# A dense layer's up products as three products of rounded halves, for the last three of eight batches

## The reference

```python
# block 1, per batch of 1024 tokens
h  = layernorm(layernorm(x), gamma, beta)
h  = spiral_conv(h)                       # a causal convolution with a decaying complex exponential
x1 = h + layernorm(x)
h  = layernorm(x1, gamma, beta)
h  = silu(h @ w1 + b1) @ w2 + b2          # the dense layer: 128 -> 512 -> 128
x  = x + (h + x1)
# block 2: mixture of 8 experts, 2 for each token
logits = layernorm(x) @ router.T
top two experts a, b of each token, probabilities by softmax over the two logits
x = x + sum over a, b of prob * (gelu(layernorm(x) @ w1[e].T + b1[e]) @ w2[e].T + b2[e])
```

## Time and profile before

| | |
|---|---|
| median of 3 runs | 464.43 us (461.4, 464.46, 464.43) |
| the profiled execution's own time | 459.44 us |
| its span, first to last instruction | 457.7 us |
| busy: PE, DVE, ACT, POOL | 378.1 us (83%), 348.2 us (76%), 320.1 us (70%), 274.5 us (60%) |
| up products L825 | 128 records, 66.9 us |
| mean granted TensorE clock, as a share of full speed | 0.922 |
| batches 5, 6 and 7 of the dense layer | up products from 180.29 to 238.6 us of the span |

### The profile page before, as it was taken

The page is one execution under the profiler, slowest core; times in us unless marked ns, Lnnn a source line. Parts: engine busy times, 40 slices in busy tenths (PEclk is TensorE's granted clock), DMA queues, the critical chain, the costliest instruction groups (busy, mean ns, idle before and its releaser), DMA issues.

```text
span 457.7 us, 11199 instructions
## 1 busy us (share of the span) xinstructions
PE 378.1 (83%) x2716; PEld 323.4 (71%) x2716; DVE 348.2 (76%) x1320; ACT 320.1 (70%) x772; POOL 274.5 (60%) x339
## 2 busy tenths in 40 slices
PE   1275188797999899898994598999999999999970
PEld 1132147484867667685774588999999999999970
DVE  7999999796989988988438158776777777777770
ACT  5783386978888797976671555777777777777740
POOL 6980756393777788776746505675555555555451
PEclk9995589998989799999998579999999999999995
DMA  7649122020222221222312233444333333333200
GB/s 252 178 145 327 53 47 47 1 46 3 58 87 47 86 60 49 79 79 67 116 37 99 75 86 102 140 148 122 108 96 99 101 98 100 111 105 102 76 3 0
DMA packets 34434, 41.60 MB, mean 91 GB/s; under 512 B 5382, under 2 KB 29459, under 8 KB 34244
## 3 DMA queue, kind: packets, MB, share of 16 engines
q1 hardware_dynamic: 27236, 23.56, 17.9%
q0 software_dynamic: 7136, 17.33, 13.1%
HBM read 19.52 MB, written 18.92 MB: 84 GB/s over the span
## 4 chain that ended last, share of the span: by engine, by line
PE 59%; DVE 17%; issue 6%; POOL 5%; ACT 4%; POOLq 0%; DVEq 0%; ACTq 0%
PE up_p L998 12%; PE down_p L836 7%; PE up_p L825 7%; PE turn_p L998 6%; PE down_p L1017 6%; PE route_p L1017 6%; PE up_p L1017 5%; PE turn_p L813 4%; DVE stats L1097 3%; PE down_p L1007 2%; DVE work L1162 2%; DVE work L1160 2%; ACT work L648 2%; POOL sorted_rows L560 2%; PE route_p L874 2%
## 5 line engine op out<-in xcount | busy, mean ns | idle before, releaser
L597 POOL DMA_INDIRECT out<-result,out_id x91 | 89.2, 980 | 90.1 <-DVE result L1475 70.9
L560 POOL DMA_INDIRECT sorted_rows<-rows,pos x64 | 73.8, 1153 | 32.8 <-issue 16.8
L825 PE MATMUL up_p<-h_t,work 128*128 128x512 f32 x128 | 66.9, 651 | 10.5 <-ACT work L622 9.3
L836 PEld LDWEIGHTS down_p<-w_sb,work 128*128 128x128 f32 x512 | 60.6, 192 | 9.7 <-issue 9.6
L998 PE MATMUL up_p<-xt,work 128*128 128x128 f32 x488 | 66.5, 281 | 0.0
L787 ACT ACTIVATE work<-mw_c 128x256 f32 x182 | 65.6, 414 | 0.3 <-issue 0.2
L836 PE MATMUL down_p<-w_sb,work 128*128 128x128 f32 x512 | 63.0, 277 | 0.0
L998 PEld LDWEIGHTS up_p<-xt,work 128*128 128x128 f32 x488 | 61.0, 196 | 0.1
L772 ACT ACTIVATE hid_t<-up_p 128x512 f32<-128x512 f32 x61 | 36.4, 597 | 30.4 <-PE up_p L998 30.3
L813 PE MATMUL turn_p<-ident,work 128*128 128x128 f32 x192 | 30.2, 309 | 29.1 <-ACT work L648 11.9
L813 PEld LDWEIGHTS turn_p<-ident,work 128*128 128x128 f32 x192 | 25.7, 161 | 37.6 <-ACT work L648 12.8
(11 more groups left out here) (236 smaller groups left out, 812.9 us busy)
## 6 DMA issues: line engine op xcount, KB each, us to landing
tin<-sorted_rows SPq DMA_DIRECT2D x91, 136.0 KB, 2.2
resid<-in_x SPq DMA_DIRECT2D x8, 512.0 KB, 3.8
resid<-work POOLq DMA_DIRECT2D x8, 512.0 KB, 4.6
sorted_rows<-zeros SPq DMA_DIRECT2D x29, 136.0 KB, 2.3
out<-result,out_id POOLq DMA_INDIRECT x91
work<-in_mw SPq DMA_DIRECT2D x1, 1024.0 KB, 6.5
sorted_rows<-rows,pos POOLq DMA_INDIRECT x64, 2.5
work<-in_w SPq DMA_DIRECT2D x1, 256.0 KB
```

The costliest lines, as they stand in the source:

```text
L560: g.indirect_dma_start(sorted_dram, bass.IndirectOffsetOnAxis(pos[b % 2][:, j:j + 1], 0), rows[b % ROWBUFS][:, j, :], None).then_inc(s_sor ...
L597: g.indirect_dma_start(out_rows, bass.IndirectOffsetOnAxis(out_id[k][:, :], 0), result[k][:, :], None, bounds_check=TOKENS - 1, oob_is_err ...
L825: t.matmul(dst, w1_g[:, k], half(h_t, h), start=True, stop=True).then_inc(s_up, 1)
L836: last = t.matmul(down_p[:, j * D:(j + 1) * D], silu[c % 2][:, j * TILE:(j + 1) * TILE], w2_sb[:, c, :], start=False, stop=c == FC - 1, sk ...
```

## The change

For batches 5, 6 and 7 (`b >= SPLIT`, `SPLIT = 5`) each float32 up product becomes three f32r products that add up in the same PSUM tile: high half of `w1` with low half of `h`, high with high, low with high. ScalarE's `high(b)` writes the rounded `h_hi` in place of `h_t`. A new operation `low(b)` on VectorE subtracts `h_hi` from `turn_p` to get `h_lo`; it stands between `x2_sum(b-1)` and `x1_sum(b+1)`, and for batch 7 between `x2_sum(6)` and its statistics. The halves of the weights are made once: `w1_hi` by ScalarE at the end of its iteration 3, `w1_lo` by VectorE at the end of its iteration 4. The first products of a batch wait for `low(b)`, and `conv_turn(b+1)`, which overwrites `turn_p`, waits for it too. `h_t` moves to a slot of `work`, and `b2_hi` shares the space of `h_lo`.

```diff
+SPLIT = 5
...
+        h_hi = sb("h_hi", [128, LENGTH], f32r)
+        h_lo = sb("h_lo", [128, LENGTH], f32r)
+        w1_hi = sb("w1_hi", [128, FF], f32r)
+        w1_lo = sb("w1_lo", [128, FF], f32r)
+        b2_hi = h_lo[0:2, 0:HALF]
...
+        h_t = slot(16)
...
-                s_.activation(h_t[:, :], turn_p[:, :], ACT.Copy).then_inc(s_hi, 1)
+                s_.activation(h_t if b < SPLIT else h_hi[:, :], turn_p[:, :], ACT.Copy).then_inc(s_hi, 1)
...
                 if live(b3):
                     x0_norm(b3)
+                if i == 3:
+                    s_.activation(w1_hi[:, :], w1_g, ACT.Copy).then_inc(s_w1hi, 1)
...
                 if c == 0:
                     pe.wait_ge(s_hi, b + 1)
+                    if b >= SPLIT:
+                        pe.wait_ge(s_lo, b + 1 - SPLIT)
+                    if b == SPLIT:
+                        pe.wait_ge(s_w1lo, 1)
...
-                    t.matmul(dst, w1_g[:, k], half(h_t, h), start=True, stop=True).then_inc(s_up, 1)
+                    if b < SPLIT:
+                        t.matmul(dst, w1_g[:, k], half(h_t, h), start=True, stop=True).then_inc(s_up, 1)
+                        continue
+                    t.matmul(dst, w1_hi[:, k], half(h_lo, h), start=True, stop=False)
+                    t.matmul(dst, w1_hi[:, k], half(h_hi, h), start=False, stop=False)
+                    t.matmul(dst, w1_lo[:, k], half(h_hi, h), start=False, stop=True).then_inc(s_up, 1)
...
                 after(pe, s_hi, b)
+                if b > SPLIT:
+                    pe.wait_ge(s_lo, b - SPLIT)
                 turned(lambda j: vi[:, j * TILE:(j + 1) * TILE], s_t2)
...
+            def low(b):
+                v.wait_ge(s_hi, b + 1)
+                after(v, s_up, b * 2 * FC)
+                d.tensor_tensor(h_lo[:, :], turn_p[:, :], h_hi[:, :].bitcast(f32), ALU.subtract).then_inc(s_lo, 1)
...
                 if live(b0):
                     x2_sum(b0)
+                if i >= SPLIT:
+                    low(i)
                 if live(b1):
                     x1_sum(b1)
...
+                if i == SPLIT - 1:
+                    v.wait_ge(s_w1hi, 1)
+                    d.tensor_tensor(w1_lo[:, :], w1_g, w1_hi[:, :].bitcast(f32), ALU.subtract).then_inc(s_w1lo, 1)
...
             x2_sum(LAST - 1)
+            low(LAST)
             x2_stats(LAST - 1)
```

More of the change, by code:

```diff
@@ L93, in block_moe_kernel @@
         ident = sb("ident", [128, 128])
-        h_t = sb("h_t", [128, LENGTH])
-        b2_hi = sb("b2_hi", [2, HALF], f32r)
+        h_hi = sb("h_hi", [128, LENGTH], f32r)
[3 more added lines that the diff above has]
+        b2_hi = h_lo[0:2, 0:HALF]
         mw1_c = sb("mw1_c", [128, EXPERTS * EF])
@@ L293, in block_moe_kernel @@
         s_hi = sem("h_turned_copied")
+        s_lo = sem("h_low_half_ready")
+        s_w1hi = sem("w1_high_ready")
+        s_w1lo = sem("w1_low_ready")
         s_up = sem("up_done")
@@ L731, in _ @@
             a.wait_ge(s_ident, 1)
-            s_.activation(b2_hi[:, :], b2_rows, ACT.Copy).then_inc(s_aw, 1)
+            s_.activation(b2_hi, b2_rows, ACT.Copy).then_inc(s_aw, 1)
             s_.activation(w1_g, w1_sb, ACT.Copy, scale=par[:, GAMMA:GAMMA + 1])
             a.wait_ge(s_aw, 1)
-            s_.activation(b2_first, b2_hi[:, :].bitcast(f32), ACT.Copy, scale=ident[0:2, 0:1]).then_inc(s_whi, 1)
+            s_.activation(b2_first, b2_hi.bitcast(f32), ACT.Copy, scale=ident[0:2, 0:1]).then_inc(s_whi, 1)
             bias_diagonals()
@@ L1302, in iteration @@
                     convolution(b2)
+                if i == SPLIT - 1:
+                    v.wait_ge(s_w1hi, 1)
+                    d.tensor_tensor(w1_lo[:, :], w1_g, w1_hi[:, :].bitcast(f32), ALU.subtract).then_inc(s_w1lo, 1)
             def weights():
                 v.wait_ge(s_whi, 1)
-                link(d.tensor_tensor(b2_lo, b2_rows, b2_hi[:, :].bitcast(f32), ALU.subtract))
+                link(d.tensor_tensor(b2_lo, b2_rows, b2_hi.bitcast(f32), ALU.subtract))
                 d.scalar_tensor_tensor(out=b2_hi_lo[:, :], in0=b2_lo, scalar=ident[0:2, 1:2], in1=b2_first,
```

## The result

The changed kernel took 463.98 us in the median of 12 runs (462.26 to 468.82), the kernel before 463.37 us in the same session (458.28 to 464.46, 12 runs). The ratio is 1.0076 with a 95% interval of 1.0041 to 1.0111, so the change makes the kernel slower by about 3.5 us. The two medians lie closer than that because both sets of times are spread over some 6 us and are not symmetric; the ratio is what I use. A second measurement of the same two kernels (`e12_changed_again`, 29 runs of the kernel before) has 463.95 us against 460.97, ratio 1.0080.

The account below looks back on a forecast made before the run. A loop over VectorE was taken to bound batches 5 and 6. Delays of 1.6 and 1.4 us made 3.0; with the clock falling, 5.4 to 6.2, taken as 5.8: 464.43 + 5.8 = 470.2 us, range 464.8 to 473.8.

Parts of the forecast that it names:

- the case that I gave 0.40: Whole kernel: measured time within 1% (4.6 us) of no change, chance 0.40.
- What bounds the kernel: TensorE is the busiest engine, yet in the stages of batches 5 and 6 a loop over VectorE sets the pace.
- VectorE, batch 5: `w1_lo`, `low` and the transposes' wait make `x1_sum` 2.1 us later; 1.6 us of delay left at the positions.
- Batch 6: `x1_sum` comes 1.4 us later and the delay passes through VectorE undiminished: 1.4 us added.
- Batch 7: `low(7)` waits for `high(7)`, products begin 0.9 us later and regain it by the third chunk: net 0.
- The halves of the weights: ScalarE's `w1_hi` copy ahead of batch 4's first silu costs 0, at most 0.6 us; VectorE's `w1_lo` takes 0.6 to 0.7.
- The products: On TensorE, 0.215 us per f32r product plus 0.42 us for the type switch; gain 2.1 us in all.
- The first reading: f32r products have twice a float32 record's column rate, leaving 0.42 us for entering and leaving the type.
- rival 3: f32r products no faster a column than float32 records, or loads in the open: +6 to +10 us, 472 to 475; chance 0.07.
- The clock: New TensorE gaps ahead of `conv_turn(6)` and `conv_turn(7)` lower the granted clock to 0.50; total delay 5.8 us, against 3.0 without.
- the likeliest case: Clock falls behind both new TensorE gaps, in batches 5 and 6: 5.8 us more, chance 0.45.
- Rival 2: Not slower: the products' saved TensorE time ends up in the result, 5.2 us less, 459.2; chance 0.06.

Follow-up runs that it names:

- e12_changed_again: The changed kernel measured and profiled once more, unaltered, against the kernel before: ratio 1.0080, median 463.95 us against 460.97.
- e1_no_low: Changed kernel without the subtraction and its waits, first product reading the high half; against the kernel before 1.0019, median 461.78 us against 460.94.
- e2_low_alone: Changed kernel with the subtraction and its waits kept but float32 up products in place of the f32r ones: ratio 1.0152 to the kernel before.
- e4_fill: Changed kernel plus ten unused f32r products ahead of conv_turn(6) and of conv_turn(7), in TensorE's gaps: ratio 1.0052 to the kernel before.
- e3_low_first: Changed kernel with low(b) moved in front of x2_sum(b-1) in iterations 5 and 6: ratio 1.0054 to the kernel before.
- e9_first_fill_all: Changed kernel with low(b) ahead of x2_sum(b-1), plus unused products: five ahead of conv_turn(6) and conv_turn(7), four ahead of batch 7: 1.0029 to the kernel before.

## Why the prediction was right, and which terms were off

The forecast was 5.8 us more and the measurement says 3.5; the direction, the place and the mechanism were as written, two sizes were not. I had put the larger chance, 0.54, on a time above 469.1 us, over 1% slower; 0.8% is the case that I gave 0.40. On the median of 464.43 that the forecast starts from, the ratio gives 468.0 us, inside the range. The changed kernel's own median of 463.98 is lower than the range's lower end of 464.8, because the start was high: it was a median of three runs, and further runs of the kernel before have medians of 463.37, 460.94, 460.64 and 460.97.

- **What bounds the kernel.** Right. VectorE's round sets the pace in batches 5 and 6. Without the subtraction the loss is gone (`e1_no_low`), with it and without the new products it doubles (`e2_low_alone`). Of the 3.9 us lost in the two stages, 1.7 came through TensorE's slower transposes, as the clock term had it.
- **VectorE, batch 5.** `w1_lo` took 0.69 us, `low` 1.21 to 1.23 us, and `x1_sum` came 5.0 us after the convolution's end where I had 4.4 for the full and 5.3 for the lower clock. In `e4_fill`, at the full clock, it was 4.2. The gap of 0.49 us before the positions was used up as said.
- **Batch 6.** `x1_sum` came 4.3 us after the convolution's end, forecast 3.65 at the full and 4.55 at the lower clock.
- **Batch 7.** I said net 0; it is -0.34 us. A chunk by itself is faster than I had it, 0.24 us less than a float32 one, which would fit; no run takes the term apart.
- **The halves of the weights.** The copy on ScalarE costs nothing as said. `w1_lo` alone costs nothing either, since it fits the gap ahead of `x1_sum`. Together with `low` there is no such gap, and I take its 0.6 us as lost there, as forecast; no run has `low` without `w1_lo` in batch 5.
- **The products.** Mis-sized. I had 0.215 us a product and 0.42 us for entering and leaving the type, 1.7 us for a chunk. The trace has 0.23 us a product, about 0.1 us on entering and nothing on leaving: 1.48 us for a chunk, 0.24 less than the float32 ones. The 0.42 us came from the two bias products, and it is theirs: right behind f32r products, with no type to enter, they still take 0.66 us (218.41 to 219.07 in the changed kernel). The first reading (twice the column rate) was the right one, and rival 3 is out. The rule of the Trainium skill ("TensorE: Matmul & The Clock Gate", "Part 3: Packing small matmuls", "The mechanism") that loads overlap products only with other row groups doesn't hold here: every one of these products has a load of its own of the full 128 rows, the loads last 0.19 us, and the products still start 0.23 us apart. The same section also says that a load to the background weight buffer is pulled ahead of running products; the trace is in line with that and not with the "only".
- **The clock.** It fell behind both new gaps in both profiles of the changed kernel, as forecast for the likeliest case. Its price was mis-sized. The forecast had 5.8 - 3.0 = 2.8 us for it, because TensorE was to be the later engine at the positions of batch 3 and at the place counting of batch 4. It was not: its stretch from `conv_turn(6)` to the next transposes took 6.1 us (187.42 to 193.54) and not 6.8, the later chunks gave back 0.24 us each, and VectorE stayed the bound. What the lower clock cost is 1.7 us (changed against `e4_fill`, both stages; 1.4 to 1.7 by the stretches ahead of `x1_sum` alone), nearly all by the longer transposes ahead of `x1_sum`, 1.94 us against 1.06. The part at the full clock was off as well: 2.2 us in `e4_fill` where I had 3.0. Of these 0.8 us, 0.34 is the spread of the stretch ahead of the convolution's end (21.92 us in `e4_fill`, 22.26 before).
- **Rival 2**, the faster one, failed where I put its deciding point: the gap of 1.12 us ahead of `x1_sum` doesn't hold the 1.21 us and a transposition. Its price was too high too. With no subtraction at all and the clock held the products give 1.66 us and not 5.2 (0.25 of the 1.66 is again the spread of the first stage).

What stays open: why the clock fell in batch 7 in the profiles of `e3_low_first` and `e4_fill` and not in the changed kernel, where the gap ahead of it is the same 0.73 us; why it fell in batch 3 behind a wait of 2.99 us in one profile and not in another; whether batch 7 alone is worth having, as one measurement says 0.9951 and the other 0.9985; and why the second phase is shorter in nine of the profiles. No experiment had the subtraction in batches 5 and 6 without a loss: a version in which `low` reads a copy, so that `conv_turn` needn't wait, would need room and time on another engine and wasn't tried.

## What to carry to other kernels

A cheaper product on the busiest engine is worth what that engine's waits leave of it; read which engine's round closes the stage before pricing the gain. An added operation that reads a shared PSUM tile also holds back the next writer of that tile, so it belongs first among its neighbours: moving `low` ahead of `x2_sum` gave back 1.85 us of the 3.9 lost in two stages. A gap opened on TensorE can cost a second time through the clock, and a gain on TensorE can open such a gap.

## What the runs showed of the hardware

- A product of f32r operands of 128x128 and 128x512 starts 0.23 us after the one before at the full clock and 0.43 us at 1.2 GHz; a float32 one takes two records of 0.43 us at the full clock.
- Filling a gap of 3.3 us with 2.55 us of products kept the clock at 1.00 although 0.89 us of it stayed empty (`e4_fill`); filling one of about 2.3 us with 1.4 us of them, with 0.91 us left empty, didn't (`e9_first_fill_all`).
- Equal waits at one place aren't always followed by the same clock: behind 2.99 us in batch 3 it fell to 0.50 in the changed kernel's profile and held at 1.00 in the one before, and that stage then took 27.41 us in place of 23.01. Behind 0.73 us in batch 7 it fell in `e3_low_first` and held in the changed kernel.
- A faster TensorE gave its gain back: in `e1_no_low` the wait of 2.62 us for VectorE was followed by the lower clock, the stage was 2.66 us longer, and nine products without a use in the gap removed both.
